# Three fused multiply-and-add instructions in place of six, in the experts' layer

## The reference

```python
q = jnp.einsum('btd,ed->bte', hidden_states, W_q)
q = q.reshape(b, t, 2, h, n).transpose(2, 0, 1, 3, 4)
sim = jnp.einsum('pbthn,hkpn->pbthk', q, keys)
scores_xy, idx_xy = jax.lax.top_k(sim, K)
sx, sy = (scores_xy[0], scores_xy[1])
ix, iy = (idx_xy[0], idx_xy[1])
all_scores = (sx[..., :, None] + sy[..., None, :]).reshape(b, t, h, K * K)
all_idx = (ix[..., :, None] * nk + iy[..., None, :]).reshape(b, t, h, K * K)
scores, pk = jax.lax.top_k(all_scores, K)
indices = jnp.take_along_axis(all_idx, pk, axis=-1)
w = jax.nn.silu(jnp.einsum('btd,bthkd->bthk', hidden_states, de) * jax.nn.softmax(scores, axis=-1))
experts_states = jnp.einsum('bthk,bthkd->btd', w, ue)
```

## Time and profile before

| | us |
|---|---|
| median of 3 runs | 4635.48 |
| the profiled execution | 4640.9 |
| its span | 4639.6 |
| DVE busy | 3884.1 (84%) |
| PE busy | 4165.6 (90%) |
| ACT busy | 3493.9 (75%) |
| POOL busy | 3561.3 (77%) |

### The profile page before, as it was taken

One profiled execution on the slowest core, in us unless ns is written; L12 is line 12 of the kernel. 1 busy time (PEld: TensorE's weight loads), 2 busy tenths in 40 slices (PEclk: granted clock), 3 DMA queues, 4 the chain that ended last, 5 costly groups with the idle time before them and its releaser, 6 DMA issues.

```text
span 4639.6 us, 140828 instructions
## 1 busy us (share of the span) xinstructions
PE 4165.6 (90%) x57664; PEld 3028.7 (65%) x57664; DVE 3884.1 (84%) x6471; ACT 3493.9 (75%) x6378; POOL 3561.3 (77%) x2624
## 2 busy tenths in 40 slices
PE   7987565558886999999999999999999999999998
PEld 5665354445663677777777777777777777777666
DVE  4665999955557999999999999999999999999994
ACT  4664788864444788888888888888888888888886
POOL 1111888863338998989898999889898999998984
PEclk9999788879997999999999999999999999999999
DMA  2000000000000222222222222222222222222222
GB/s 63 2 2 1 1 1 1 1 20 9 2 2 15 53 55 53 67 64 62 54 62 63 58 55 53 63 63 64 55 63 63 58 55 53 63 62 60 52 59 60
DMA packets 120845, 198.83 MB, mean 43 GB/s; under 512 B 66896, under 2 KB 78224, under 8 KB 120080
## 3 DMA queue, kind: packets, MB, share of 16 engines
q1 hardware_dynamic: 120208, 189.82, 16.5%
HBM read 24.12 MB, written 2.10 MB: 6 GB/s over the span
## 4 chain that ended last, share of the span: by engine, by line
PE 73%; DVE 10%; issue 6%; POOL 6%; ACT 5%; DMA 0%; DVEq 0%; POOLq 0%; SPq 0%; ACTq 0%
PE ps L1306 8%; PE ps L1250 7%; PE ps L1317 7%; PE ps L1251 7%; PE ps L1278 5%; PE ps L1259 5%; PE ps L1290 4%; PE ps L1297 4%; PE ps L1298 3%; PE ps L1358 3%; PE ps L1347 3%; PE ps L1341 2%; PE ps L1272 2%; DVE arena L598 2%; PE ps L344 2%
## 5 line engine op out<-in xcount | busy, mean ns | idle before, releaser
L1585 POOL TENSOR_TENSOR arena<-arena 128x32 f32<-128x32 f32 x192 | 1058.2, 5511 | 233.9 <-DVE arena L1498 233.9
L1590 POOL TENSOR_TENSOR arena<-arena 128x1024 f32<-128x1024 f32 x384 | 907.4, 2363 | 7.2 <-DVE arena L1489 7.2
L208 POOL TENSOR_SCALAR arena<-arena 128x2 f32<-128x2 f32 x256 | 72.3, 282 | 633.5 <-DVE arena L202 622.2
L1608 POOL TENSOR_TENSOR arena<-arena 128x1536 f32<-128x1536 f32 x192 | 529.1, 2755 | 24.1 <-DVE arena L1522 24.1
L1488 DVE TENSOR_TENSOR arena<-ps,arena 128x1024 f32<-128x1024 f32 x384 | 462.1, 1203 | 73.1 <-ACT arena L1376 68.7
L1376 ACT ACTIVATE arena<-ps 128x1024 f32<-128x1024 f32 x384 | 394.6, 1028 | 124.4 <-PE ps L1251 119.3
L1397 ACT ACTIVATE arena<-arena 128x96 f32<-128x96 f32 x1536 | 427.6, 362 | 75.0 <-DVE arena L1514 74.9
L1489 DVE TENSOR_TENSOR arena<-ps,arena 128x1024 f32<-128x1024 f32 x384 | 466.1, 1214 | 0.0
L1306 PEld LDWEIGHTS ps<-arena 96*64 96x64 f32 x12288 | 384.2, 137 | 112.6 <-issue 112.4
L1496 DVE TENSOR_REDUCE arena<-arena 128x32 f32<-128x2048 f32 x192 | 436.8, 2275 | 0.0
L1406 ACT ACTIVATE arena<-ps 96x1024 f32<-96x1024 f32 x384 | 390.0, 1016 | 59.6 <-PE ps L1290 58.9
(11 more groups left out here) (252 smaller groups left out, 9992.3 us busy)
## 6 DMA issues: line engine op xcount, KB each, us to landing
arena<-arena SPq DMA_DIRECT2D x192, 384.0 KB, 4.3
arena<-arena SPq DMA_DIRECT2D x192, 256.0 KB, 3.7
arena<-arena SPq DMA_DIRECT2D x192, 128.0 KB, 2.3
arena<-in_dWqkv SPq DMA_DIRECT2D x18, 512.0 KB, 3.9
arena<-arena SPq DMA_DIRECT2D x96, 64.0 KB
arena<-arena SPq DMA_DIRECT2D x96, 63.5 KB
arena<-in_dWo SPq DMA_DIRECT2D x6, 512.0 KB, 4.1
arena<-in_x SPq DMA_DIRECT2D x4, 512.0 KB, 7.5
```

Source lines behind the costliest of these rows:

```text
L1585: pool.tensor_tensor(ss[:, 0:32], ss[:, 32:64], mhalf32, ALU.pow).then_inc(*S.rs.up())
L1590: pool.tensor_tensor(a1[:, half], a1[:, half], T2[:, half], ALU.add).then_inc(*radd[g].up())
L1608: pool.tensor_tensor(P, P, bc(SM[n % 3][:, 2, :], 2, 96), ALU.mult).then_inc(*S.pn.up())
```

## The change

Each of the three steps was a scaling in place followed by an addition with a wait between them. Now each is one instruction with two operations, the multiplication by an immediate and the addition of the second operand. It waits for the step before it as the scaling did. The values are small whole numbers and the weights powers of two, so both forms give the same numbers.

```diff
                 e = T.eq
                 dve.wait_ge(*eq[t].at(b + 1))
                 for n, w in ((1024, 16.0), (512, 4.0), (256, 2.0)):
-                    dve.tensor_scalar(e[:, 0:n], e[:, 0:n], w, None, ALU.mult).then_inc(*S.step_dve.up())
-                    dve.wait_ge(*S.step_dve.now())
-                    dve.tensor_tensor(T.R if n == 256 else e[:, 0:n], e[:, 0:n], e[:, n:2 * n], ALU.add
-                                      ).then_inc(*(tr[t] if n == 256 else S.step_dve).up())
+                    dve.scalar_tensor_tensor(T.R if n == 256 else e[:, 0:n], e[:, 0:n], w, e[:, n:2 * n], ALU.mult, ALU.add
+                                             ).then_inc(*(tr[t] if n == 256 else S.step_dve).up())
                     if n > 256:
                         dve.wait_ge(*S.step_dve.now())
```

## The result

The changed kernel took 4652.12 us (median of 7 runs, 4646.8 to 4652.23) against 4635.48 before (7 runs, 4633.46 to 4639.71). The ratio is 1.0033, with a 95% interval from 1.0023 to 1.0042: slower by 15 us, between 11 and 19. The medians lie 16.6 us apart. The forecast was 4647.5, slower by 12 us.

A forecast was written before the change was run, and what follows sets the result against it. A once-per-batch cycle of waits through POOL, ACT and DVE was taken to bound phase_b. 10.9 plus 0.8, less 0.9, plus 1.5 gave 12.3 us more; 12.0 on the median is 4647.5, range 4627 to 4656.

The forecast's parts named there:

- The fused form's rate: DVE's fused steps in phase_b: one element a cycle, three taking 2.34 us free of POOL against 2.36 for six.
- The extra 0.02 us of fixed time: Added to each fused instruction on DVE; counted as 0.06 us in 25 places, 1.5 us more.
- The rule of the holds: DVE and POOL work on shared operands one at a time; the second starts about 0.135 us before the first's recorded end.
- the first place: Tile A's steps in phase_b, ahead of L198: POOL's path 0.78 us longer, counted 14 times, 10.9 us.
- second place: Tile B's steps in phase_b, ahead of L1038: DVE 0.10 us sooner, counted in 9 batches, 0.9 us less.
- The start-up term: First two batches at tile A's steps: half the usual delay, 2 x 0.39 = 0.8 us more.
- The other batches: Behind the first batches: 0.78 us more each at tile A's steps, 0.10 less at tile B's in 9.
- the second rival, absorbed: POOL's delay in phase_b half made up in gaps between DVE's holds: 5 to 7 us more, 4641; chance 0.22.
- Two elements a cycle: First rival, DVE's fused steps in phase_b: 11.6 us less, 4624; chance 0.11.
- The count of instructions: Third rival, three fewer DVE instructions per tile: 4.3 us less, or 24 less (4611) with DVE as bound; chance 0.08.
- Slower than one a cycle: Fourth rival, fused form on DVE at two cycles an element: 1.9 us more per tile, some 50 us; chance 0.03.

The follow-up runs named there:

- the two cut versions: a_first and a_split, both against the kernel before: tile A's 1024-element step alone fused, or all of tile A fused with that step halved; 1.0021 of before each.
- a_split: Against the kernel before: tile A's three steps fused, the 1024-element one cut into two of 512, tile B old; 1.0021 of before.
- b_only: Against the kernel before: fused steps in tile B only, the old six instructions in tile A; 0.9996 of before.
- a_first: Against the kernel before: only tile A's 1024-element step fused, its other steps and all of tile B old; 1.0021 of before.
- first3: Against the kernel before: fused steps in both tiles of the first three batches only, old steps in the other 13; 1.0016 of before.

## Why the prediction was right, and where not

**The fused form's rate** was right: 0.42 us for 256 elements free, and the three together take 2.40 us where POOL is not in the way (509.40), the predicted 2.34 and two gaps of 0.03. The extra 0.02 us of fixed time, 1.5 us of the sum, is not there. This agrees with section 5.1 of the Trainium skill's "Vector Engine (DVE) Microarchitecture Reference", in whose list of modes the operation is missing.

**The rule of the holds** was right, and carried further than the forecast: 0.80 more for L208 at the first place (0.78 predicted), 0.12 less at the second (0.10), and the two cut versions within 0.03 us. The Trainium skill's "SBUF — State Buffer", section "Who interferes with whom", says that a DVE instruction with two SBUF inputs contends with a GpSimd instruction that reads SBUF. The trace agrees: L1109 takes 1.22 us beside the first fused step, where it had 0.42. The 0.135 us by which the one starts ahead of the other's recorded end comes from the rows before alone.

**The start-up term** was wrong. For the first three batches the sum held 0.39 + 0.39 + 0.78 and 0.2 of fixed time, 1.8 us; measured are 5.3 (83.0 - 77.7). The step that failed is "In the first two DVE has no idle time behind trB, and I count half". It looked at whether DVE had room, and not at where POOL's next operations would land: in three long holds of DVE.

**The other batches** were wrong by about as much to the other side. From the third second place to the end the sum held 13 x 0.78 - 0.9 + 1.3 = 10.5 us, where 1.3 is the extra fixed time; measured are 5.9 (1045.77 - 547.52 less 1033.68 - 541.30). The distances show it: from first to second place 8.8 us more over 13 batches, since in five of them POOL was further ahead (11.33, 11.56, 11.56, 12.31 and 12.30 us in place of 12.50) and met other pieces. Against that, the one batch of before in which POOL was further ahead (9.87 us) takes 12.50 now, 2.63 more, where the prediction took the same 0.78 for it. From second to first place it is 2.1 us less, where 0.9 was counted, and the last stretch 0.8 less. This is a part of the second rival, absorbed, beside the forecast. The total of 12.3 against 11.1 is thus closer than its parts: a start-up that is 3.5 us too low and other batches that are 4.6 too high cancel, and that is luck. What was right is the direction, the place and the 0.8 us of one first place.

**The rivals.** Two elements a cycle fell with the first row of the new line. The count of instructions fell with the result itself and with `a_split`, where one instruction more cost less. Slower than one a cycle fell too.

**The names** of the two places were swapped. I had taken the tile of each from the neighbours in the trace and not from the table, in which eqA (842) and trA (894) stand ahead of eqB (1178) and trB (1298). The sum doesn't use the letters, but two expectations were turned round by it.

## What to carry to other kernels

Where two engines share a path to memory, compare instructions by how long each holds it, and not only by their own time: three instructions of 2.34 us replaced six of 2.36, and the kernel lost 0.33%, because the other engine could slip in five times before and twice after. Before a fusion, look up at each of its places which engine is on the path; here it paid at one of two, and there by so little that only the profile shows it. And the order of the pieces was worth more than these instructions: with two pieces moved the kernel gained 0.46%. But moving only the one behind the wait that the profile named, DVE's 1.75 us for ACT, took that wait away and made the kernel 0.12% slower.

## What was not expected of the hardware

One rule with one constant, fitted on two rows, gave the shifts at the two places to 0.05 us in the changed kernel, `b_only`, `a_first` and `a_split`. In the second batch a delay of 0.8 us on POOL became one of 2.3 us at the end of r0, and ACT's L909 waited 4.36 us for it in place of 1.57, when each of POOL's next operations came just behind the start of a longer one on DVE. Of the 5.0 us that the first three batches cost in `first3`, 1.5 were made up in the batches behind them.
